# Decoder layer on one core: the score matmuls of the heads written as four column tiles of 32 keys

## The reference

```python
q = x @ Wq
latent_kv = (k + v) @ W_down_kv
k_rec = latent_kv @ W_up_k
v_rec = latent_kv @ W_up_v
qh, kh, vh = (heads(q), heads(k_rec), heads(v_rec))
scores = jnp.einsum('bhqd,bhkd->bhqk', qh, kh) * scale
decay = jnp.exp(-LAMBDA_DECAY * TIME_STEP * jnp.abs(idx[:, None] - idx[None, :]))
scores = scores * decay[None, None, :, :]
attn = jax.nn.softmax(scores, axis=-1)
out = jnp.einsum('bhqk,bhkd->bhqd', attn, vh)
```

## Time and profile before

| | us |
|---|---|
| median of 3 runs | 871.83 (870.6 to 872.9) |
| the profiled execution, its span | 871.3 |
| ACT's 256 exponentials, of 1.113 each | 283.0 busy |
| PE's 704 score matmuls | 156.3 busy |
| PE's 2048 value matmuls | 164.0 busy |
| heads, first score matmul to the last values | 125.5 to 423 |

### The profile page before, as it was taken

One profiled execution on the slowest core, in us unless ns is written; L12 is line 12 of the kernel. 1 busy time (PEld: TensorE's weight loads), 2 busy tenths in 40 slices (PEclk: granted clock), 3 DMA queues, 4 the chain that ended last, 5 costly groups with the idle time before them and its releaser, 6 DMA issues.

```text
span 871.3 us, 14935 instructions
## 1 busy us (share of the span) xinstructions
PE 688.6 (79%) x4414; PEld 348.5 (40%) x4415; DVE 356.6 (41%) x1005; ACT 421.2 (48%) x503; POOL 226.7 (26%) x245
## 2 busy tenths in 40 slices
PE   0899329999999999999767899998728187888860
PEld 0444103333333333333454466666714155555530
DVE  2329943333333433333144355552372033333353
ACT  2134239999999999999423233332400022222100
POOL 2035519719607900000010100000017500000265
PEclk9999859999999999999889899995559589999985
DMA  9500034555555554555260000000002323333235
GB/s 293 201 0 0 1 65 76 84 88 86 82 89 87 84 88 82 89 88 106 85 200 13 1 1 0 0 0 0 1 6 104 106 66 98 109 109 111 88 107 157
DMA packets 55379, 66.50 MB, mean 76 GB/s; under 512 B 10994, under 2 KB 46964, under 8 KB 55348
## 3 DMA queue, kind: packets, MB, share of 16 engines
q1 hardware_dynamic: 52276, 57.73, 29.8%
q0 software_dynamic: 3072, 8.39, 3.1%
HBM read 22.04 MB, written 18.87 MB: 47 GB/s over the span
## 4 chain that ended last, share of the span: by engine, by line
PE 67%; DVE 12%; issue 6%; SPq 5%; DMA 3%; another core or an unknown queue 2%; ACT 2%; DVEq 2%; POOL 1%; POOLq 0%; ACTq 0%
PE ps L650 15%; PE ps L638 14%; PE ps L909 6%; PE ps L783 4%; PE ps L763 3%; SPq L346 3%; PE ps L863 3%; PE ps L537 2%; PE ps L924 2%; PE ps L733 2%; PE ps L797 2%; PE ps L530 2%; PE ps L901 1%; PE ps L798 1%
## 5 line engine op out<-in xcount | busy, mean ns | idle before, releaser
L1056 ACT ACTIVATE pT<-ps,shift 128x1024 f32<-128x1024 f32 x256 | 283.0, 1113 | 19.4 <-PE ps L650 11.0
L638 PE MATMUL ps<-qstack,kstack 96*128 96x512 bf16 (+3 forms) x704 | 156.3, 327 | 11.4 <-DMA kstack<-parts 11.3
L650 PE MATMUL ps<-pT,vcur 128*32 128x256 f32 x2048 | 164.0, 392 | 0.7 <-ACT pT L1056 0.7
L1354 DVE TENSOR_TENSOR ps<-ps,within 128x128 f32<-128x128 f32 x256 | 76.7, 300 | 184.2 <-PE ps L638 184.1
L638 PEld LDWEIGHTS ps<-qstack,kstack 96*128 96x128 bf16 x704 | 48.4, 98 | 110.4 <-issue 77.0
L650 PEld LDWEIGHTS ps<-pT,vcur 128*32 128x32 f32 x2048 | 40.3, 108 | 89.2 <-issue 53.6
L909 PE MATMUL ps<-parts,oT 128*128 x192 | 55.6, 414 | 17.6 <-ACT oT L1172 12.4
L513 POOL DMA_INDIRECT val<-y_slots,place_i x32 | 31.2, 975 | 143.3 <-DMA y_slots<-ftmp 129.8
L505 POOL DMA_INDIRECT x_slots<-val,place_i x32 | 31.5, 984 | 90.0 <-DVE place_i L1574 80.6
L1177 ACT ACTIVATE xnT<-ps 128x128 f32<-128x128 f32 x48 | 13.3, 277 | 80.0 <-PE ps L909 80.0
L909 PEld LDWEIGHTS ps<-parts,oT 128*128 128x128 f32 x192 | 33.7, 195 | 38.9 <-issue 36.0
(11 more groups left out here) (231 smaller groups left out, 987.4 us busy)
## 6 DMA issues: line engine op xcount, KB each, us to landing
qstack<-parts SPq DMA_DIRECT2D x192, 64.0 KB, 2.3
kstack<-parts SPq DMA_DIRECT2D x192, 64.0 KB, 2.5
x_slots<-wcur SPq DMA_DIRECT2D x1, 6144.0 KB, 20.6
kT<-x_slots SPq DMA_DIRECT2D x48, 128.0 KB, 2.0
y_slots<-ftmp SPq DMA_DIRECT2D x48, 128.0 KB, 1.7
resid<-in_x_dram SPq DMA_DIRECT2D x4, 512.0 KB, 5.4
parts<-in_L_ffn_Wg_dram SPq DMA_DIRECT2D x16, 128.0 KB, 2.2
parts<-in_L_ffn_Wu_dram SPq DMA_DIRECT2D x16, 128.0 KB, 2.3
```

The source lines that it names most:

```text
L638: mm = nc.tensor.matmul(ps[:, score_bank(g3, kt) + g, a - lo:z - lo], kstack[:, r, 1 - sign, kt * P:(kt + 1) * P], qstack[:, r, sign, a:z] ...
L650: mm = nc.tensor.matmul(ps[2 * HD * g:2 * HD * (g + 1), 6 + r, 0:256], vcur[:, r, kt, :], pT[:, kt % 2, 256 * g:256 * (g + 1)], start=(kt ...
L1056: nc.scalar.activation(pT[:, kt % 2, :], two_banks(score_bank(g3, kt)).rearrange("p a n -> p (a n)"), ACT.Exp, bias=shift[:]).then_inc(s_e ...
L1354: nc.vector.tensor_tensor(blk, blk, within[:], ALU.mult).then_inc(s_diag, 1)
```

## The change

Each score matmul of 128 keys becomes four of 32 keys. Each has 32 columns of weights from `kstack`, streams the same queries, and writes its 32 PSUM partitions on the column tile of the array at the same place, as the value matmuls do. The signal `s_fs` stays on the last one of each bank.

```diff
                     cut = min(max(kt * P, lo), hi)
                     for a, z, sign in ((lo, cut, 0), (cut, hi, 1)):
                         if a < z:
-                            mm = nc.tensor.matmul(ps[:, score_bank(g3, kt) + g, a - lo:z - lo],
-                                                  kstack[:, r, 1 - sign, kt * P:(kt + 1) * P],
-                                                  qstack[:, r, sign, a:z], start=True, stop=True)
+                            for c in range(4):
+                                keys32 = slice(kt * P + 32 * c, kt * P + 32 * (c + 1))
+                                mm = nc.tensor.matmul(ps[32 * c:32 * (c + 1), score_bank(g3, kt) + g, a - lo:z - lo],
+                                                      kstack[:, r, 1 - sign, keys32], qstack[:, r, sign, a:z],
+                                                      start=True, stop=True, tile_position=(0, 32 * c))
                     mm.then_inc(s_fs, 1)
```

## The result

The changed kernel takes **886.3 us**, the median of four runs (881.3 to 889.5), beside 871.2 for the kernel before on the same chip (870.2 to 872.9): a ratio of 1.016 (1.014 to 1.019), slower. The forecast was 878.4. The sign, the mechanism and the range held; the loss is twice the forecast one, +1.6% for +0.8%, which is the size of three terms, the clock's above all. The profiled execution has a span of 884.0.

What follows compares the result with a forecast made beforehand. PE's chain was taken to bound the heads, with ACT and the loads close behind: 871.3 - 11.9 + 1.3 = 860.7 us with code held, plus 8.7, 7.5 and 1.5 if not, 878.4 us; range 857 to 889.

Steps and rivals of the forecast that it cites:

- (1): PE's steps: two gaps of 0.09 us at changes between score and value form go; two changes per head stay.
- (4): Heads: period 8.755 us against 9.14, set by two alternating load buffers; 31 heads save 11.9 us.
- (7): Later loop passes, code not held: instruction packets, 1.25 per head over 24 heads at 0.29 us each, +8.7 us.
- (8): PE's loop: four taken branches to code that isn't there, 2.8 us each, a third covered, +7.5 us.
- (9): After PE's stops in the loop: a lower granted clock, 0 to 2 us each, taken as +1.5 us in all.
- (6): First loop pass: 308/176 as many instruction packets, 4.5 more, +1.3 us.
- (3): H, from a head's first score to SP's next issue, falls from 8.67 to 7.9 us (7.6 to 8.2).
- stagger: Added start delay of the four column-tile score matmuls, 0.03 us per burst of scores; PE's step becomes 0.96 us.
- (5): PE's code: matmuls and weight loads per head grow from 176 to 308, the six-head loop from 1056 to 1848.
- A: Rival: PE's longer loop is still held, 861 us (856 to 866), chance 0.27.
- C: Rival: only the loop's first block is lost, four stops and few packets, 869.7 us (866 to 873), chance 0.13.
- D: Rival: PE is limited by issuing 19 matmuls per step, 885 to 905 us, chance 0.06.

Runs made afterwards that it cites:

- a_l2: The changed kernel with score banks by kt % 3 (an extra wait) and PE's loop of two heads instead of six: 854.1 us, 0.981 of the kernel before.
- a_unroll: The changed kernel with PE's loop over 30 heads written out, so no branch back: 861.9 us, 0.996 of the kernel before.
- b_l2: The kernel before with score banks by kt % 3 (an extra wait) and PE's loop of two heads: 878.3 us, 1.007 of the kernel before.
- a_l6: The changed kernel with score banks by kt % 3 (an extra wait), PE's loop still of six heads: 890.7 us, 1.023 of the kernel before.
- b_unroll: The kernel before with PE's loop over 30 heads written out, banks as before: 869.0 us, 1.004 of the kernel before.
- a_l2_rows5: `a_l2` with five rows of products instead of six, so ten DMAs a head, not twelve: 843.5 us, 0.974 of the kernel before.

## Why the prediction was right in sign and wrong in size

| piece, us | forecast | measured | from |
|---|---|---|---|
| 24 heads with the code held, terms (1) to (4) | -9.2 | -11.1 | `a_l2` less before |
| packets in later passes, (7) | +8.7 | +10.7 | 38 at 0.28, `a_unroll` less `a_l2` |
| four back branches, (8) | +7.5 | +9.6 | PE stands 12.1 longer than in `a_unroll`, less 2.5 for 9 packets |
| the clock, (9) | +1.5 | +7.7 | PE is busy 7.7 longer than in `a_unroll` |
| the first heads and the other stages, with (6) | -1.4 | -4.2 | the rest of the span |
| span | 878.4 | 884.0 | 871.3 and the above |

**The step that failed is the size of (9), the clock behind the stops, and less so of (8), the back branch.** Together they were put at 9.0 us and came to 17.3. For (9) I took 1.5 us in all, out of 0 to 2 for each stop; measured are 7.7, about 1.9 a stop, at the top of that span. PE works at a granted clock of 0.50 for 4.3 us or more behind two of the stops and at 0.68 for 3.4 behind the two others, and at 0.50 again at head 10. The earlier trace rows had it: a clock of 0.50 over 4 us costs up to 2 us of work. For (8) I took 2.8 us a stop with a third covered; PE stands 3.12 to 4.48, 3.7 in the mean, 14.8 in all, and 9.6 remain, so the cover of a third held and the stop was too short. The same row misled there: the jump after the heads stood 3.09 for one packet, and I called that a bound from above, where the loop's stops are longer. SP's next load waits for the scores that the stop made late, so a stop comes back two heads on (head 10's 1.67 above); that is in these numbers.

**(7) was 2 us low.** The price held, 0.28 a packet for 0.29, but 38 came in the 24 heads and not 30. Two cautions. `a_l2` has the extra wait, which `a_unroll` lacks; on the kernel before it costs 5.8 us in 24 heads (`b_l2`), on the changed one 7.2 (`a_l6`, 243.8 for 236.6). Were held heads with the old banks faster by so much, the gain of the first row would be up to 7 us larger, a packet would cost up to 0.53, and 2 us of the 17.3 would pass from the branches to the packets. That kernel can't be had with a loop of two heads, so this wasn't tried. And packets cost less in the kernel before: the 16 of `b_unroll` 5.6 us in the same 24 heads, 0.35 each, but by the ratio of whole runs 3.2 us, 0.20 each.

**(1) to (3) held, and were a little low.** PE's step is 0.87, not 0.96: a gap is (1.11 - 0.87) / 2 = 0.12, not 0.09, and no stagger shows. H is 7.76 in `a_l2` (head 18's first score at 287.17 to SP's issue at 294.93), for 7.9 forecast. **(4) was right by 0.1, in part by luck:** 8.66 for 8.755, but set by ACT and PE in turn and not by the loads, since heads with shorter loads (`a_l2_rows5`) take 8.66 as well. ACT's floor is 1.00, where the forecast read 1.05 from the earlier trace rows.

**(5), (6) and the choice held.** Packets came much as forecast: 11 for 9.5 from 130 to 200 us, 34 for about 30 later, with stops at heads 8, 14, 20 and 26. In (6) stands a slip: by its five packets, 308/176 as many are 3.75 more and not 4.5, +1.1 us for +1.3. A, "held", fails for this kernel; `a_l2` shows what it would have been, 854 to 855 for 861. C fails by the 34 packets. D fails: 19 matmuls in 0.87 us are 0.046 each. The Trainium skill's 0.062 for decoding in a program (TensorE: Matmul & The Clock Gate) would give the step 1.18 us, so the trace disagrees with it.

Had (7), (8) and (9) been taken at their measured 28.0, the same sum would have given 889; the held heads and the stages outside give 5 us back.

## What to carry to other kernels

A change that multiplies an engine's instructions in a loop is to be priced twice, by what the instructions do and by whether the loop is still held; instruction packets on q8 in later passes and idle time on "issue" at each return are the signs. Then shorten the loop before giving up the form: here the same matmuls went from 1.6% slower to 1.9% faster by looping over two heads, not six, and even writing all heads out beats a loop that isn't held. And where a row shows a similar stop, look also at what the clock did behind it, and price that once for every stop: here the lower clock cost nearly as much as the standing.

## What the runs showed of the hardware

- PE's loop of some 1520 instructions was brought once; one of 1913 brought 38 packets of 16 KB in four later passes, 9.5 a pass, and with its start to be aligned to a block 36. Straight code brought a packet per 255 to 264 matmuls and weight loads (`a_unroll` 29, `b_unroll` 16 in 24 heads).
- Each return cost PE 3.1 to 4.5 us of standing and 3.4 us or more at a lower granted clock, about 4 us net by estimate. In the 24 heads of straight code PE never stood over 1.44 us, what was over 1 us was a wait for a load, and the mean granted clock was 1.00.
- Column tiles of 32 that follow tiles of 32 have no gap between bf16 scores and fp32 values (0.87 us for four waves of 0.22). Tiles of 64 next to tiles of 32 have the full one (0.56 + 0.57 us a step, as before).
- Exponentials of 128 x 1024 that wait for nothing start 1.00 to 1.01 us apart, though each shows 1.11.
- The mark on the branch back had no effect that the runs show (886.8 us for 886.3).
